# Attention and mixture-of-experts layer on one core: router on centred rows, weight splits behind the slots, zeros ahead of the weights, TensorE on ones while x arrives

## The chip, the cores and the metric

One Trainium2 chip, one of its cores. Its engines run their own instruction streams and wait for each other through semaphores: TensorE (PE; its weight loads PEld), VectorE (DVE), ScalarE (ACT), GpSimd (POOL) and SyncE (SP), which here only issues DMAs. The metric is the device time of one execution in microseconds (us). All numbers below come from the runs and from one profiled execution of this kernel.

## What is computed

x has 8 x 256 tokens of 128 channels, float32. After a layer norm without weights, the result feeds two branches, and the sum goes to the output:

```
xn  = layernorm(x)                                  # (8, 256, 128)
out = x + attn(xn) + ffn(xn)
attn: xq = layernorm(xn) * norm_g + norm_b;  q = xq @ Wq;  k, v = split(xn @ Wkv)
      two null keys and values per head; q, k scaled to length 1 (q_scale, k_scale)
      softmax(8 * q k^T + slope_h * -|i - j|, causal) @ v, 16 heads of 64;  @ Wout
ffn:  shared  = (silu(xn @ sg_w.T) * (xn @ su_w.T)) @ sd_w.T
      probs   = sigmoid(xn @ router_w.T + routing_bias)    # 8 experts
      top 2 per token, weights p / sum(p)
      routed  = sum over the two experts e of w_e * (silu(xn @ wg[e].T) * (xn @ wu[e].T)) @ wd[e].T
```

So there are two norms of tokens: xn (here "first norm", scale `rstd[0]`) and the norm of xn ("second norm", `nmean[1]`, `rstd[1]`).

## The kernel before, in words

Tokens lie on 128 partitions in NT = 16 tiles of 128. The kernel has three parts.

The prologue (0 to about 90 us). SP issues x as one DMA (L316), then wg and wu (L317), wd, the shared weights, Wq, Wkv and Wout, and last three writes of zeros to `slot_x` in DRAM (L328), where each expert's tokens get padded slots. ScalarE's queue issues nine small DMAs counted by one semaphore (`small_in`, L523 to L526; the router's weights and bias are the last two). VectorE takes the mean of x and writes the centred rows `xc` (L713 to L715), ScalarE squares them (L537), VectorE reduces the squares, GpSimd raises the variance to the power -0.5 (L388), VectorE multiplies: `xn1` (L729). In between TensorE transposes the first EARLY = 4 of 14 weight groups (L945), ScalarE writes the rounded high part (L534) and VectorE the rest (L710) of each. TensorE then transposes `xn1` in four groups of four tiles (`tokens_turned`, L949), ScalarE copies them to `xn1T` (L544), and small float32 matmuls with the transposed router weights `rwT` give the logits (`logits`, L957). VectorE adds the bias (L744), ScalarE takes tanh (L548), and a chain of some 60 short VectorE instructions (L747 to L782) finds the two best experts and each token's two places: `slot`; `tile_expert` follows (L784 to L787). TensorE gives the ranks in between (L976, L977).

Then GpSimd scatters the rows of `xn1` to their slots in DRAM with 32 indirect DMAs (`scatter(n)`, L403, loop L498), one after the other on its queue. In front of scatter 15 it waits until the second norm's rows are turned (`t_ev`, L499), and at 15 and 22 it also splits the first 256 tokens of `xn2T` and `xn1T` in two parts (`entry("ahead", ...)`, L445 and L448), from which TensorE computes the first keys and queries ahead (`entry("ahead")`, L1093). The second norm runs on VectorE (L732 to L737) and GpSimd (L392 to L398), and its rows are turned behind the ranks (L978). After that come the null keys and values (L791, L982 to L990, L563 to L565) and the ten other weight groups (L991 on TensorE, L566 on ScalarE, L795 on VectorE), then the subtractions for Wq and Wkv (L798, L799). A group's transposes wait for the evacuation of the group four before it (`w_lo`, L939).

The expert loop (about 90 to 165 us): SP waits for all scatters and for the split of Wq and Wkv (L331, L332), then loads 39 tiles of slots one by one. The batches (the rest): eight passes of 16 heads, on all engines; in each, GpSimd gathers the experts' rows (L494) and scales keys and queries by their norms (L414 to L430).

The semaphore waits that matter: `consts` (GpSimd's constants, 5), `poolc` (its first fills), `rstd_ready`, `xn1_ready`, `slots_ready`, `zero_in`. TensorE's queue is in order: what it does ahead of the tokens, the tokens wait for.

## Time and profile before

| | us |
|---|---|
| median of three runs | 515.41 (513.67 to 516.01) |
| the profiled execution | 515.42 |
| its span (first to last instruction) | 513.7 |

| engine | busy us, share of the span |
|---|---|
| TensorE | 427.9 (83%) |
| VectorE | 374.2 (73%) |
| ScalarE | 356.2 (69%) |
| GpSimd | 327.0 (64%) |

```profile
PE   0557324899998899998998999899899899989985
DVE  3754354465653798788889888888978888897884
POOL 3284787960000598867968968896796888677140
PEclk9997757799999999999999999999999999999999
DMA  7950111222222000001000000100000000010010
```

One digit is the busy share, in tenths, of one of 40 equal slices (12.8 us each). The first seven slices are the prologue, in which no engine but GpSimd is busy for long; the expert loop and the batches follow. PEclk is the granted clock in tenths of full speed, 9 standing for 90% or more; of its two levels, 1.0 is 2.4 GHz and 0.5 is 1.2 GHz. Busy shares are means over stages with different limits, so the prologue is read from the chain of waits and the timelines, whose times count from the span's start. In them "L941" is a line of the kernel, "x16" the number of instructions merged into the row, and the bracket gives the idle time before it and what ended it. GpSimd's times are rough.

### The profile page before, as it was taken

Reading aid. Unit: us, or ns where it says so; the run is one execution under the profiler, and the core shown is the slowest. Engines: PE = TensorE matmul, PEld = TensorE weight load, DVE = VectorE, ACT = ScalarE, POOL = GpSimd, SP = SyncE. Lnnn points to the kernel's source line nnn. Section 1 sums busy time; section 2 is a strip of 40 time slices with the busy share of each in tenths; the row PEclk is TensorE's granted clock in tenths of the full one; section 3 lists DMA queues with packets and bytes.
Section 4 is the critical chain, followed back from the end, with each engine's and each line's share of the span. In section 5 each row is a group of like instructions: output and inputs, shape, how many; then the busy total and the mean of one; then the engine's idle time right before and its main releaser. Section 6 shows DMA issues by size and latency. Waiting matters only on the chain.

```text
span 513.7 us, 11688 instructions
## 1 busy us (share of the span) xinstructions
PE 427.9 (83%) x2793; PEld 305.6 (59%) x2793; DVE 374.2 (73%) x1401; ACT 356.2 (69%) x1091; POOL 327.0 (64%) x492
## 2 busy tenths in 40 slices
PE   0557324899998899998998999899899899989985
PEld 0555212577777566665665666666567566656663
DVE  3754354465653798788889888888978888897884
ACT  1433124466666887886897897889789788869854
POOL 3284787960000598867968968896796888677140
PEclk9997757799999999999999999999999999999999
DMA  7950111222222000001000000100000000010010
GB/s 218 349 156 27 51 36 52 57 76 74 73 79 58 1 1 22 2 3 36 8 0 20 20 0 10 31 0 0 26 15 0 20 20 0 0 36 5 2 42 11
DMA packets 28159, 21.04 MB, mean 41 GB/s; under 512 B 3512, under 2 KB 25312, under 8 KB 28000
## 3 DMA queue, kind: packets, MB, share of 16 engines
q1 hardware_dynamic: 25264, 16.46, 10.8%
q0 software_dynamic: 2048, 4.20, 2.7%
q8 instruction: 13, 0.21, 0.2%
q10 hardware_dynamic: 816, 0.03, 0.1%
q14 instruction: 18, 0.15, 0.1%
HBM read 12.41 MB, written 8.26 MB: 40 GB/s over the span
## 4 chain that ended last, share of the span: by engine, by line
PE 30%; POOL 23%; issue 16%; DVE 14%; ACT 8%; DMA 6%; ACTq 1%; POOLq 1%; SPq 1%; DVEq 1%; another core or an unknown queue 0%
POOL slot_x L404 6%; POOL rnorm L414 4%; PE bank L928 4%; POOL arena_b L494 4%; PE bank L1138 3%; PE bank L929 3%; PE bank L930 3%; DVE arena_b L858 3%; DMA arena_b<-slot_x 3%; DVE arena_b L835 3%; ACT arena_b L646 3%; PE bank L1061 2%; POOL rpow L417 2%; DMA arena_b<-in_L_ffn_wu_dram 2%; PE bank L1070 2%
## 5 line engine op out<-in xcount | busy, mean ns | idle before, releaser
L646 ACT ACTIVATE arena_b<-arena_b,nmx 128x130 f32<-128x130 f32 (+1 forms) x256 | 114.9, 457 | 29.4 <-DVE nmx L858 16.8
L858 DVE CUSTOM_DVE_ANT_0 arena_b<-bank,bias 128x130 f32<-128x130 f32 (+1 forms) x256 | 81.1, 354 | 28.7 <-ACT arena_b L646 14.5
L873 DVE TENSOR_SCALAR arena_b<-arena_b,rden 128x130 f32<-128x130 f32 (+1 forms) x256 | 87.0, 384 | 4.5
L417 POOL TENSOR_TENSOR rpow<-ssm,mhalf 128x8 f32<-128x8 f32 x32 | 53.1, 1659 | 35.2 <-DVE ssm L846 34.5
L1061 PE MATMUL bank<-ident,arena_b 128*128 128x128 f32 x384 | 67.0, 283 | 9.3 <-DVE arena_b L873 9.3
L430 POOL TENSOR_TENSOR arena_b<-arena_b,rnorm 128x512 f32<-128x512 f32 x64 | 66.8, 1044 | 8.4 <-POOL rnorm L420 3.8
L1061 PEld LDWEIGHTS bank<-ident,arena_b 128*128 128x128 f32 x384 | 43.8, 141 | 28.9 <-DVE arena_b L873 20.3
L1070 PE MATMUL bank<-arena_a 64*128 64x130 f32 (+1 forms) x512 | 59.5, 351 | 0.8 <-ACT arena_a L607 0.8
L414 POOL TENSOR_TENSOR rnorm<-ssm,mhalf 128x8 f32<-128x8 f32 x32 | 52.9, 1654 | 0.0
L584 ACT ACTIVATE arena_b<-bank 128x512 f32<-128x512 f32 x64 | 38.1, 595 | 19.7 <-PE bank L930 19.0
L646 ACT ACTIVATION_READ_ACCUMULATOR arena_b<-arena_b,nmx 128x1 f32 x256 | 50.9, 199 | 0.0
L842 DVE TENSOR_REDUCE ssq<-arena_b 128x8 f32<-128x512 f32 x64 | 43.6, 681 | 7.1 <-ACT arena_b L584 5.6
L1016 PE MATMUL bank<-ident,arena_b 128*128 128x128 f32 x256 | 39.8, 279 | 6.9 <-ACT arena_a L593 5.0
L1051 PE MATMUL bank<-probT,arena_a 128*64 128x256 f32 x256 | 43.4, 404 | 2.0 <-ACT oT L626 1.0
L404 POOL DMA_INDIRECT slot_x<-arena_a,slot x32 | 33.2, 1038 | 15.6 <-issue 9.2
L1016 PEld LDWEIGHTS bank<-ident,arena_b 128*128 128x128 f32 x256 | 28.9, 140 | 20.9 <-issue 14.5
L494 POOL DMA_INDIRECT arena_b<-slot_y,slot_now x32 | 32.3, 1010 | 13.8 <-issue 7.3
L1070 PEld LDWEIGHTS bank<-arena_a 64*128 64x128 f32 x512 | 33.6, 186 | 12.4 <-issue 8.9
L883 DVE COPY probT<-bank 128x384 f32<-128x384 f32 x64 | 35.5, 554 | 7.3 <-PE bank L1061 2.3
L445 POOL CAST arena_r<-xn2T 128x256 fp32r (+1 forms) x8 | 3.2, 398 | 56.2 <-PE bank L930 56.2
L1084 PE MATMUL bank<-oT,wo 128*128 128x256 f32 x128 | 38.2, 380 | 0.0
L585 ACT ACTIVATE arena_b<-bank 128x512 f32<-128x512 f32 x64 | 38.0, 593 | 0.0
(202 smaller groups left out, 1032.4 us busy)
## 6 DMA issues: line engine op xcount, KB each, us to landing
slot_x<-probT SPq DMA_DIRECT2D x3, 832.0 KB, 9.9
arena_b<-slot_x SPq DMA_DIRECT2D x39, 64.0 KB, 1.9
slot_y<-arena_b SPq DMA_DIRECT2D x39, 64.0 KB, 1.5
arena_b<-in_L_ffn_wd_dram SPq DMA_DIRECT2D x1, 1024.0 KB, 9.5
arena_b<-in_L_attn_Wkv_dram SPq DMA_DIRECT2D x1, 1024.0 KB, 8.8
arena_b<-in_L_attn_x_dram SPq DMA_DIRECT2D x8, 128.0 KB, 2.1
out_dram<-arena_b SPq DMA_DIRECT2D x8, 128.0 KB, 1.8
arena_b<-in_L_attn_Wq_dram SPq DMA_DIRECT2D x1, 512.0 KB, 6.4
```

The lines of the kernel that those rows point to most:

```text
L404: pool.indirect_dma_start(xg_dram, bass.IndirectOffsetOnAxis(ap=slot[:, n // TOPK, n % TOPK:n % TOPK + 1], axis=0), xn1[:, n // TOPK, :], ...
L414: gp.tensor_tensor(rnorm[:, j, :], ssm[:, j, :], mhalf[:, 0:HEADS // 2], ALU.pow).then_inc(g.r_ready, 1)
L417: gp.tensor_tensor(rpow[:, j, :], ssm[:, j, :], mhalf[:, 0:HEADS // 2], ALU.pow).then_inc(g.pw, 1)
L430: gp.tensor_tensor(rows, rows, bc(rnorm[:, j, :], DH), ALU.mult).then_inc(g.kqn, 1)
L494: pool.indirect_dma_start(yg[:, t, c, :], None, yg_dram, bass.IndirectOffsetOnAxis(ap=slot_now[:, t, c:c + 1], axis=0)).then_inc(g.gath, 16)
L646: sc.activation(prob[:, h % 4, c], sim[h % 2][:, c], ACT.Exp, scale=-1.0, bias=nmx[:, h % HEADS, t:t + 1], accum_out=den[:, h % HEADS, t:t ...
L842: ve.reduce_sum(ssq[j % 2][:], sqb[j % 2].rearrange("p (h d) -> p h d", d=DH), AX.X).then_inc(g.red, 1)
L858: ve.tensor_tensor_reduce(out=sim[h % 2][:, c], in0=bank[h % 2][:, c], in1=bias[:, c], scale=-SLOPES[h], scalar=3e38, op0=ALU.add, op1=ALU ...
L873: ve.tensor_scalar(pr, pr, rden[:, h % HEADS, t:t + 1], None, ALU.mult).then_inc(g.pn, 1)
L1016: ins = te.transpose(side[i][:, q * P:(q + 1) * P], src[:, p * P:(p + 1) * P], ident[:])
L1061: ins = te.transpose(bank[2 + h % 2][:, k * P:(k + 1) * P], prob[:, h % 4, c:c + P], ident[:])
L1070: ins = te.matmul(bank[half][:, c0:c1], qT[r, h // 2, q0:q0 + P], kT[r, h // 2, 0:c1 - c0], start=True, stop=True)
```

## The change

- **x** arrives in two DMAs (tiles 0 to 7, 8 to 15). Behind them SP issues the zero writes and only then the weights. The router's weights are the first small DMA, with their own semaphore; the bias is next among the small ones.
- **Ones.** Before anything else, TensorE runs WARM = 72 bf16 matmuls of the tile `ones` with itself into a bank that nobody reads.
- **Router on centred rows.** Statistics and centring run in halves. TensorE turns `xc` instead of `xn1`, ScalarE copies it to `xn2T` (free at that time), and the router's matmuls have a ninth column of ones, so that the sum of a centred row comes with its logits. VectorE multiplies the sums by `rstd[0]`, adds the bias, and takes the second norm's mean from the ninth column.
- **First norm's rows.** Half 0 on VectorE, half 1 on GpSimd; they are turned after the router and copied to `xn1T` (now evacuations 5 to 8).
- **Second norm.** Its variance is computed on GpSimd; its rows by 16 VectorE instructions with two scalars, into `x_all`; turned last (evacuations 9 to 12).
- **Weights.** All 14 groups are transposed and split behind the slots, the first four included, as are the small steps for the null keys. The null keys' power goes from GpSimd's early part to the place in front of scatter 8. In front of scatter 15, GpSimd waits for evacuation 12 instead of 8.

Context lines are left out; the list of semaphores, too.

```diff
+WARM = 72
...
-rw_raw, rwT = sb("rw_raw", [E, DIM]), sb("rwT", [P, E])
+rw_raw, rwT = sb("rw_raw", [E, DIM]), sb("rwT", [P, E + 1])
...
-sync.dma_start(x_all, xv).then_inc(g.x_in, 16)
+sync.dma_start(x_all[:, 0:NT // 2, :], xv[:, 0:NT // 2, :]).then_inc(g.x_in0, 16)
+sync.dma_start(x_all[:, NT // 2:NT, :], xv[:, NT // 2:NT, :]).then_inc(g.x_in1, 16)
+sync.wait_ge(g.nvz, 1)
+zv = xg_dram.rearrange("(p r) d -> p r d", p=P)
+for i in range(0, SLOT_TILES, 13):
+    sync.dma_start(zv[:, i:i + 13, :], zeros.unsqueeze(1).to_broadcast([P, 13, DIM])).then_inc(g.zero_in, 16)
...
-sync.wait_ge(g.nvz, 1)
-zv = xg_dram.rearrange("(p r) d -> p r d", p=P)
-for i in range(0, SLOT_TILES, 13):
-    sync.dma_start(zv[:, i:i + 13, :], zeros.unsqueeze(1).to_broadcast([P, 13, DIM])).then_inc(g.zero_in, 16)
...
+gp.memset(rwT[:, E:E + 1], 1.0).then_inc(g.poolc, 1)
...
-pool.wait_ge(g.poolc, 27)
+pool.wait_ge(g.poolc, 28)
...
-pool.wait_ge(g.var_ready, 1)
-gp.tensor_tensor(rstd[0][:], var[0][:], mhalf[:, 0:NT], ALU.pow).then_inc(g.rstd_ready, 1)
-pool.wait_ge(g.n_sm, 1)
-gp.tensor_tensor(nr[:], nsm[:], mhalf[0:32, 0:1], ALU.pow).then_inc(g.n_r, 1)
-pool.wait_ge(g.var_ready, 2)
-gp.tensor_tensor(rstd[1][:], var[1][:], mhalf[:, 0:NT], ALU.pow).then_inc(g.rstd_ready, 1)
...
-    gp.tensor_tensor(xc[:, tt, :], xn1[:, tt, :], bc(nmean[1][:, tt], DIM), ALU.add).then_inc(g.xc2_ready, 1)
-    pool.wait_ge(g.xc2_ready, half + 1)
-    pool.wait_ge(g.rstd_ready, 2)
-    gp.tensor_tensor(x_all[:, tt, :], xc[:, tt, :], bc(rstd[1][:, tt], DIM), ALU.mult).then_inc(g.xn2_ready, 1)
+    pool.wait_ge(g.var_ready, half + 1)
+    gp.tensor_tensor(rstd[0][:, tt], var[0][:, tt], mhalf[:, tt], ALU.pow).then_inc(g.rstd_ready, 1)
+tt = slice(NT // 2, NT)
+pool.wait_ge(g.xc1_ready, 2)
+pool.wait_ge(g.rstd_ready, 2)
+gp.tensor_tensor(xn1[:, tt, :], xc[:, tt, :], bc(rstd[0][:, tt], DIM), ALU.mult).then_inc(g.xn1b_ready, 1)
+pool.wait_ge(g.nm2_ready, 1)
+gp.tensor_tensor(vsum[1][:], nmean[1][:], nmean[1][:], ALU.mult).then_inc(g.pchain, 1)
+gp.tensor_tensor(var[1][:], vsum[0][:], rstd[0][:], ALU.mult).then_inc(g.pchain, 1)
+pool.wait_ge(g.pchain, 2)
+gp.tensor_tensor(var[1][:], var[1][:], rstd[0][:], ALU.mult).then_inc(g.pchain, 1)
+pool.wait_ge(g.pchain, 3)
+gp.tensor_scalar(var[1][:], var[1][:], 1.0 / DIM, LN_EPS, ALU.mult, ALU.add).then_inc(g.pchain, 1)
+pool.wait_ge(g.pchain, 4)
+gp.tensor_tensor(var[1][:], var[1][:], vsum[1][:], ALU.subtract).then_inc(g.pchain, 1)
+pool.wait_ge(g.pchain, 5)
+gp.tensor_tensor(rstd[1][:], var[1][:], mhalf[:, 0:NT], ALU.pow).then_inc(g.rstd_ready, 1)
...
+    if n == 8:
+        pool.wait_ge(g.n_sm, 1)
+        gp.tensor_tensor(nr[:], nsm[:], mhalf[0:32, 0:1], ALU.pow).then_inc(g.n_r, 1)
...
-        pool.wait_ge(g.t_ev, 8)
+        pool.wait_ge(g.t_ev, 12)
...
+act.dma_start(rw_raw[:], a["L0_ffn_router_w"]).then_inc(g.rw_in, 16)
...
+act.dma_start(rbias[:], a["L0_ffn_routing_bias"].rearrange("(o e) -> o e", o=1).to_broadcast([P, E])).then_inc(g.small_in, 16)
...
-act.dma_start(rw_raw[:], a["L0_ffn_router_w"]).then_inc(g.small_in, 16)
-act.dma_start(rbias[:], a["L0_ffn_routing_bias"].rearrange("(o e) -> o e", o=1).to_broadcast([P, E])).then_inc(g.small_in, 16)
...
-act.wait_ge(g.xc1_ready, 1)
-sc.activation(sq0, xc, ACT.Square).then_inc(g.sq_ready, 1)
+def squares(half):
+    tt = slice(half * NT // 2, (half + 1) * NT // 2)
+    act.wait_ge(g.xc1_ready, half + 1)
+    sc.activation(sq0[:, tt, :], xc[:, tt, :], ACT.Square).then_inc(g.sq_ready, 1)
+def turned_out(i):
+    act.wait_ge(g.t_ps, i + 1)
+    cols = slice(i % 4 * 512, (i % 4 + 1) * 512)
+    ps = bank[4 + i % 2][:]
+    if i < 8:
+        sc.activation((xn2T if i < 4 else xn1T)[:, cols], ps, ACT.Copy).then_inc(g.t_ev, 1)
+    else:
+        sc.activation(xn2T[:, cols], ps, ACT.Identity, scale=g_col[:, 0:1], bias=b_col[:, 0:1]).then_inc(g.t_ev, 1)
+act.wait_ge(g.rw_ps, 1)
+sc.activation(rwT[:, 0:E], bank[7][:, 0:E], ACT.Copy).then_inc(g.rw_ev, 1)
+squares(0)
+turned_out(0)
+squares(1)
+for i in range(1, 4):
+    turned_out(i)
+act.wait_ge(g.lg_ready, 1)
+sc.activation(lth, lg, ACT.Tanh, scale=0.5).then_inc(g.lth_ready, 1)
+for i in range(4, 8):
+    turned_out(i)
...
-act.wait_ge(g.rw_ps, 1)
-sc.activation(rwT[:], bank[7][:, 0:E], ACT.Copy).then_inc(g.rw_ev, 1)
-for i in range(4):
-    act.wait_ge(g.t_ps, i + 1)
-    sc.activation(xn1T[:, i * 512:(i + 1) * 512], bank[4 + i % 2][:], ACT.Copy).then_inc(g.t_ev, 1)
...
-act.wait_ge(g.lg_ready, 1)
-sc.activation(lth, lg, ACT.Tanh, scale=0.5).then_inc(g.lth_ready, 1)
...
-act.wait_ge(g.small_in, 16 * 9)
-for i in range(4):
-    act.wait_ge(g.t_ps, 4 + i + 1)
-    sc.activation(xn2T[:, i * 512:(i + 1) * 512], bank[4 + i % 2][:], ACT.Identity,
-                  scale=g_col[:, 0:1], bias=b_col[:, 0:1]).then_inc(g.t_ev, 1)
+for n in range(EARLY, len(groups)):
+    split_group(n)
+act.wait_ge(g.small_in, 16 * 8)
+for i in range(8, 12):
+    turned_out(i)
...
-for n in range(EARLY, len(groups)):
-    split_group(n)
...
-dve.wait_ge(g.x_in, 16)
-link(ve.reduce_sum(xsum[0][:], x_all, AX.X))
-link(ve.tensor_scalar(nmean[0][:], xsum[0][:], -1.0 / DIM, None, ALU.mult))
-ve.tensor_tensor(xc, x_all, bc(nmean[0][:], DIM), ALU.add).then_inc(g.xc1_ready, 1)
-dve.wait_ge(g.sq_ready, 1)
-link(ve.reduce_sum(vsum[0][:], sq0, AX.X))
-ve.tensor_scalar(var[0][:], vsum[0][:], 1.0 / DIM, LN_EPS, ALU.mult, ALU.add).then_inc(g.var_ready, 1)
-dve.wait_ge(g.small_in, 16 * 9)
-link(ve.tensor_tensor(nsq[:], nraw[:, 0, :], nraw[:, 0, :], ALU.mult))
-link(ve.reduce_sum(nss[:], nsq[:], AX.X))
-ve.tensor_scalar(nsm[:], nss[:], L2_EPS2, None, ALU.max).then_inc(g.n_sm, 1)
-for n in range(EARLY):
-    split_group(n)
-dve.wait_ge(g.rstd_ready, 1)
-dve.wait_ge(g.xc1_ready, 1)
+for half, arrived in ((0, g.x_in0), (1, g.x_in1)):
+    tt = slice(half * NT // 2, (half + 1) * NT // 2)
+    dve.wait_ge(arrived, 16)
+    link(ve.reduce_sum(xsum[0][:, tt], x_all[:, tt, :], AX.X))
+    link(ve.tensor_scalar(nmean[0][:, tt], xsum[0][:, tt], -1.0 / DIM, None, ALU.mult))
+    ve.tensor_tensor(xc[:, tt, :], x_all[:, tt, :], bc(nmean[0][:, tt], DIM), ALU.add).then_inc(g.xc1_ready, 1)
...
-    ve.tensor_tensor(xn1[:, tt, :], xc[:, tt, :], bc(rstd[0][:, tt], DIM), ALU.mult).then_inc(g.xn1_ready, 1)
-dve.wait_ge(g.xn1_ready, 2)
-link(ve.reduce_sum(xsum[1][:], xn1, AX.X))
-link(ve.tensor_scalar(nmean[1][:], xsum[1][:], -1.0 / DIM, None, ALU.mult))
-link(ve.tensor_tensor(vsum[1][:], nmean[1][:], nmean[1][:], ALU.mult))
-link(ve.scalar_tensor_tensor(out=var[1][:], in0=vsum[0][:], scalar=1.0 / DIM, in1=rstd[0][:], op0=ALU.mult, op1=ALU.mult))
-link(ve.tensor_tensor(var[1][:], var[1][:], rstd[0][:], ALU.mult))
-ve.scalar_tensor_tensor(out=var[1][:], in0=var[1][:], scalar=LN_EPS, in1=vsum[1][:], op0=ALU.add,
-                        op1=ALU.subtract).then_inc(g.var_ready, 1)
-link(ve.tensor_scalar(kdim[:], qsc[:], SIM_SCALE, None, ALU.mult))
-ve.tensor_tensor(kdim[:], kdim[:], ksc[:], ALU.mult).then_inc(g.kdim_ready, 1)
-ve.tensor_copy(nv2[:, 0, :], nraw[:, 1, :]).then_inc(g.n2_ready, 1)
-ve.tensor_copy(nv2[:, 1, :], nraw[:, 1, :]).then_inc(g.n2_ready, 1)
+    dve.wait_ge(g.sq_ready, half + 1)
+    link(ve.reduce_sum(vsum[0][:, tt], sq0[:, tt, :], AX.X))
+    ve.tensor_scalar(var[0][:, tt], vsum[0][:, tt], 1.0 / DIM, LN_EPS, ALU.mult, ALU.add).then_inc(g.var_ready, 1)
+dve.wait_ge(g.rstd_ready, 1)
+dve.wait_ge(g.xc1_ready, 2)
+tt = slice(0, NT // 2)
+ve.tensor_tensor(xn1[:, tt, :], xc[:, tt, :], bc(rstd[0][:, tt], DIM), ALU.mult).then_inc(g.xn1a_ready, 1)
+dve.wait_ge(g.rstd_ready, 2)
...
-ve.tensor_tensor(lg, bank[6][:, 0:NT * E].rearrange("p (t e) -> p t e", e=E), front(rbias[:], NT),
-                 ALU.add).then_inc(g.lg_ready, 1)
+dve.wait_ge(g.small_in, 16 * 8)
+sums = bank[6][:, 0:NT * (E + 1)].rearrange("p (t e) -> p t e", e=E + 1)
+link(ve.tensor_tensor(lgs[:], sums[:, :, 0:E], bc(rstd[0][:], E), ALU.mult))
+ve.tensor_tensor(lg, lgs[:], front(rbias[:], NT), ALU.add).then_inc(g.lg_ready, 1)
+ve.scalar_tensor_tensor(out=nmean[1][:], in0=sums[:, :, E], scalar=-1.0 / DIM, in1=rstd[0][:], op0=ALU.mult,
+                        op1=ALU.mult).then_inc(g.nm2_ready, 1)
...
+for n in range(EARLY):
+    split_group(n)
+link(ve.tensor_tensor(nsq[:], nraw[:, 0, :], nraw[:, 0, :], ALU.mult))
+link(ve.reduce_sum(nss[:], nsq[:], AX.X))
+ve.tensor_scalar(nsm[:], nss[:], L2_EPS2, None, ALU.max).then_inc(g.n_sm, 1)
+link(ve.tensor_scalar(kdim[:], qsc[:], SIM_SCALE, None, ALU.mult))
+ve.tensor_tensor(kdim[:], kdim[:], ksc[:], ALU.mult).then_inc(g.kdim_ready, 1)
+ve.tensor_copy(nv2[:, 0, :], nraw[:, 1, :]).then_inc(g.n2_ready, 1)
+ve.tensor_copy(nv2[:, 1, :], nraw[:, 1, :]).then_inc(g.n2_ready, 1)
+dve.wait_ge(g.rstd_ready, 3)
+dve.wait_ge(g.xn1b_ready, 1)
+dve.wait_ge(g.nm2_ready, 1)
+for t in range(NT):
+    ve.tensor_scalar(x_all[:, t, :], xn1[:, t, :], nmean[1][:, t:t + 1], rstd[1][:, t:t + 1],
+                     ALU.add, ALU.mult).then_inc(g.xn2_ready, 1)
+for n in range(EARLY, len(groups)):
+    split_group(n)
...
-for n in range(EARLY, len(groups)):
-    split_group(n)
...
+pe.wait_ge(g.poolc, 2)
+for _ in range(WARM):
+    te.matmul(bank[3][:, 0:P], ones[:], ones[:], start=True, stop=True)
...
-for n in range(EARLY):
-    transpose_group(n)
-pe.wait_ge(g.small_in, 16 * 9)
+pe.wait_ge(g.rw_in, 16)
...
-    src = xn1 if i < 4 else x_all
+    src = (xc, xn1, x_all)[i // 4]
...
-        ins = te.matmul(bank[6][:, k * E:(k + 1) * E], xn1T[:, k * P:(k + 1) * P], rwT[:], start=True, stop=True)
+        ins = te.matmul(bank[6][:, k * (E + 1):(k + 1) * (E + 1)], xn2T[:, k * P:(k + 1) * P], rwT[:],
+                        start=True, stop=True)
...
-pe.wait_ge(g.xn1_ready, 1)
+pe.wait_ge(g.xc1_ready, 1)
...
-pe.wait_ge(g.xn1_ready, 2)
+pe.wait_ge(g.xc1_ready, 2)
...
+pe.wait_ge(g.xn1a_ready, 1)
+tokens_turned(4)
+tokens_turned(5)
+pe.wait_ge(g.xn1b_ready, 1)
+tokens_turned(6)
+tokens_turned(7)
...
-for i in range(4, 8):
-    pe.wait_ge(g.xn2_ready, i // 2 - 1)
+for n in range(len(groups)):
+    transpose_group(n)
+for i in range(8, 12):
+    pe.wait_ge(g.xn2_ready, 4 * (i - 7))
...
-for n in range(EARLY, len(groups)):
-    transpose_group(n)
```

## Rows read from the trace of the kernel before

**Rows 1.** Chain that ended last, in order of time, first 140 us: start, us, what
```profile
16.05 3.66 PE bank L941 x16
...
29.38 3.23 PE bank L960 x16
...
43.74 1.24 POOL slot_x L404
```

**Rows 2.** Windows: stretch, length, busy us of each engine, granted clock, DMA share, GB/s
```profile
3.00:5.00 2.00, 0.00 (x0) 0.00 (x0) 0.00 (x0) 0.00 (x0) 1.52 (x7) 1.00 0.92 288
...
5.00:7.00 2.00, 0.00 (x0) 0.00 (x0) 0.00 (x0) 0.14 (x1) 0.00 (x0) 1.00 0.95 250
```

**Rows 3.** Timeline of VectorE, first two operations: start, us, operation, count, idle before
```profile
7.62 2.29 DVE L713 TENSOR_REDUCE xsum<-arena_a 128x16 f32<-128x2048 f32 x1 [7.62 <-DMA arena_a<-in_L_attn_x_dram]
...
10.15 2.29 DVE L715 TENSOR_TENSOR arena_a<-arena_a,nmean 128x2048 f32<-128x2048 f32 x1
```

**Rows 4.** Timeline of GpSimd up to 90 us
```profile
17.00 2.94 POOL L388 TENSOR_TENSOR rstd<-var,mhalf 128x16 f32<-128x16 f32 x1 [12.31 <-DVE var L718]
...
19.92 0.55 POOL L390 TENSOR_TENSOR nr<-nsm,mhalf 32x1 f32<-32x1 f32 x1
...
29.64 1.90 POOL L395 TENSOR_TENSOR arena_a<-arena_a,nmean 128x1024 f32<-128x1024 f32 x1
...
62.64 0.41 POOL L445 CAST arena_r<-xn2T 128x256 fp32r<-128x256 f32 x1
...
88.75 1.68 POOL L417 TENSOR_TENSOR rpow<-ssm,mhalf 128x8 f32<-128x8 f32 x1
```

**Rows 5.** Timelines of ScalarE and TensorE, first 45 us
```profile
12.48 1.91 ACT L537 ACTIVATE arena_a<-arena_a 128x2048 f32<-128x2048 f32 x1 [4.33 <-DVE arena_a L715]
...
23.39 0.60 ACT L544 ACTIVATE xn1T<-bank 128x512 f32<-128x512 f32 x1 [2.99 <-PE bank L954]
...
39.73 1.56 ACT L553 ACTIVATE xn2T<-bank,b_col,g_col 128x512 f32<-128x512 f32 x2 [4.66 <-PE bank L954]
...
22.24 1.97 PE L954 MATMUL bank<-ident,arena_a 128*128 128x128 f32 x8 [2.34 <-DVE arena_a L729]
```

**Rows 6.** Timeline of VectorE, 32 to 45 us
```profile
32.63 0.29 DVE L744 TENSOR_TENSOR arena_a<-bank,rbias 128x128 f32<-128x128 f32 x1 [5.43 <-PE bank L960]
...
33.30 0.29 DVE L747 TENSOR_SCALAR arena_a<-arena_a 128x128 f32<-128x128 f32 x1 [0.38 <-ACT arena_a L548]
...
44.59 0.37 DVE L787 CAST tile_expert<-tef 128x39 int32<-128x39 f32 x1
```

**Rows 7.** Timelines of VectorE and GpSimd beside each other, scatters and batch loop
```profile
69.14 2.28 DVE L799 TENSOR_TENSOR wkv_lo<-arena_b,wkv_hi 128x2048 fp32r<-128x2048 f32 x1
...
69.23 3.04 POOL L404 DMA_INDIRECT slot_x<-arena_a,slot  x1 [0.30 <-issue]
...
304.83 0.55 DVE L873 TENSOR_SCALAR arena_b<-arena_b,rden 128x130 f32<-128x130 f32 x2
...
317.15 2.10 DVE L835 SCALAR_TENSOR_TENSOR arena_b<-arena_b,w_now 128x128 f32<-128x128 f32 x4 [0.17 <-DVE arena_b L828]
...
318.06 1.04 POOL L430 TENSOR_TENSOR arena_b<-arena_b,rnorm 128x512 f32<-128x512 f32 x1 [0.16 <-POOL rnorm L414]
```

**Rows 8.** Weight groups: VectorE by line, timelines of VectorE and TensorE, one window
```profile
L707 DVE COPY ed<-bank 128x512 f32<-128x512 f32 x4 | 2.8, 691 | 7.9 <-PE bank L941 4.3 <-remote 3.5
...
51.51 0.69 DVE L710 TENSOR_TENSOR egu_lo<-bank,egu_hi 128x512 fp32r<-128x512 f32 x1 [0.81 <-issue]
...
60.86 0.69 DVE L707 COPY ed<-bank 128x512 f32<-128x512 f32 x1 [2.16 <-PE bank L941]
...
67.67 0.42 DVE L710 TENSOR_TENSOR sd_lo<-bank,sd_hi 128x256 fp32r<-128x256 f32 x1 [0.52 <-issue]
...
55.13 1.46 PE L941 MATMUL bank<-ident,arena_b 128*128 128x128 f32 x8 [0.71 <-issue]
...
52.00:54.00 2.00, 1.99 (x17) 1.64 (x16) 1.55 (x3) 1.17 (x3) 1.51 (x2) 0.99 0.11 37
```

6 lines of the change are left out of this document (4 added, 2 removed).

## The prediction

> **What bounds the kernel now.** I read the page first, then the chain of waits over the first 140 us, then the timelines of VectorE, GpSimd, ScalarE and TensorE up to the expert loop. The page shows no bottleneck engine for the whole span; the chain shows what the prologue hangs on. In it, TensorE waits for the weights wg and wu (16.05 us), turns them, then the tokens wait for that, and the 32 little router matmuls end at 32.6 us; 43.74 us is the first scatter [rows 1]. From there 32 scatters run one after the other on GpSimd to 88.7 us [rows 4], and the expert loop can't start before the last one has landed. VectorE, ScalarE and TensorE have gaps during all of this. So the time is: start of the first scatter, plus some 45 us of GpSimd queue, plus a rest (experts and eight batches) that the diff leaves alone. The change is worth what it moves the first scatter, minus what it adds to GpSimd's queue between scatter 0 and scatter 31.
>
> **x comes in two halves.** x is 1.05 MB. The windows give 288 GB/s from 3 us and 250 GB/s after [rows 2]: half of x is moved by 4.8 us, all of it by 6.9 us. The first reader started at 7.62 us [rows 3], 0.7 us behind the bytes, so the first half is usable at 5.5 us. The three zero writes now follow x on SP's queue in place of wg; what follows x is different, not more, so I take the second half at 7.6 us as before. Every weight waits behind the zeros: 2.6 MB at 300 GB/s or so is 8.5 us, which puts wg and wu near 24 us. VectorE's first split is now at 30 us, so this is hidden; if it were not, it would cost what the splits come late. The total of bytes is the same.
>
> **Statistics.** VectorE: the reduction and the subtraction take 2.29 us each for 2048 columns [rows 3], so about 1.2 us for a half. With the small step between (0.2 us): centred half 0 at 8.1, half 1 at 10.8 us. ScalarE's square is 1.91 us whole [rows 5], 1.0 us a half: half 0 done by 10, half 1 at 11.9. VectorE reduces the squares 10.85 to 12.0 and 12.1 to 13.3, variance ready at 12.2 and 13.45. The power on 16 columns took 2.94 us, on 8 columns 1.68 us [rows 4]: GpSimd ends at 13.9 and 15.6 us.
>
> **Router on centred rows.** It no longer waits for the power or for the weights. ScalarE copies four banks (0.60 us each [rows 5]): the second at 12.4 behind the square of half 1, the last at 14.2 if TensorE is quick, 15.0 if slow. Then four matmuls. TensorE turned 8 tiles in 1.97 us before, 0.23 us each [rows 5], and the 16 last router matmuls took 3.23 us, 0.20 us each [rows 1]. At that pace the router sums are complete at 16.0 us. [...]
>
> **A collision that the change creates.** At 15.6 us GpSimd starts the normalisation of half 1, 1.9 us for 128x1024 [rows 4], and VectorE starts the multiplication of the logits. The next VectorE instruction adds the bias with both inputs in SBUF (before, one was in PSUM [rows 6]). What such a pair does stands in the batch loop: four VectorE instructions with two SBUF inputs each took 2.10 us together, where four of the 128x130 kind beside them would take 1.1, and they ended only after GpSimd's 1.04 us multiplication at 318.06 had ended [rows 7]. So I let the bias wait for GpSimd: ready at 17.9 instead of 16.3 us. The Trainium skill, "SBUF — State Buffer", section "Who interferes with whom", says that a VectorE instruction with two SBUF inputs and a GpSimd one that reads SBUF exclude each other for the whole instruction. By that rule, too, it is 1.6 us; the trace agrees.
>
> **From the logits to the first scatter.** Before: logits added at 32.63, next step at 33.30, scatter at 43.74 [rows 1, 6]: 10.44 us, unchanged in the diff. After: next step at 18.25, first scatter at 28.7 us. GpSimd's second statistics (five small ones and a 2.9 us power) end near 22.5 us and are hidden, as the zeros are. **The first scatter moves by 15.0 us.**
>
> **GpSimd's queue between the scatters.** New there: the null keys' power, 0.55 us [rows 4], with its gap 0.65 us, on the path in full. The VectorE step it needs is done by 34 us, it stands at 39. The 16 normalisations on VectorE (two of 130 and 258 columns take 0.55 us [rows 7], so some 0.21 each) are 3.4 us; I take no cost for the scatters beside them. One scatter took 3.04 instead of 0.96 us, beside the 2.28 us subtraction of wkv [rows 7]. That subtraction still falls among the scatters, so this stays; between 2 us less and 1.2 us more, by where a scatter begins.
>
> **The wait in front of scatter 15.** It stood at 62.64 us [rows 4], for evacuations that were over 19 us earlier. Now it is for the twelfth evacuation, behind all 14 weight groups, and 17 scatters queue behind it. Due: 28.7 + 18.9 + 0.65 = 48.25 us. The chain: slots' last step 29.95 (before 44.59 + 0.37 [rows 6]), four splits at 0.66 to 32.6, small ones to 33.8, normalisations to 37.2, ten splits at 0.69 [rows 8] with TensorE at 0.9 us a group (four of the 0.23 us) to 44.0, four token groups to 46.9 us (each evacuation 0.78 us [rows 5]). That is in time by 1.3 us. But before, the same ten groups took from 51.51 to 68.09 us, 16.6 us where I count 6.8, and VectorE stood idle for 7.9 us in front of the four copies of ed, put down mostly to TensorE, although TensorE's rows show their transposes issued by 56 us [rows 8]. I can't explain these 9.8 us; they fell inside the scatters. Taken at 0, the wait costs nothing; at 9.8, it costs 8.5. New here is that the chain also contains the groups behind. I take half, 4.9 us late, so 3.6 us of stall.
>
> What follows TensorE's last token group (null keys, wo, the subtractions for Wq and Wkv) is needed at the latest when GpSimd has split the second rows at scatter 22. That comes seven scatters and one split, over 10 us, behind the wait; I estimate that work at some 9 us from its place before, and a little more is covered too, because the last scatter is released by none of it. The last scatter stays last.
>
> **Sum.** 15.0 - 0.65 - 3.6 = 10.75 us less. The profiled execution took 515.42 us (span 513.7, 1.7 us around it), the median is 515.41, so no correction: 504.6 us, span 502.9.
>
> **Rivals.** (A) As above, 504.6 us. (B) The weight chain is in time: 501.1. For it, every instruction in the chain is short and TensorE has been warmed; against it, the unexplained 9.8 us. (C) Besides, bias and GpSimd don't collide: 499.5. Against it stand rows 7. (D) The 9.8 us come back whole: 509.5. (E) The wait in front of scatter 15 turns the gain over. The six groups from the first copy of ed and the four token groups, ten in all, start at 37.9 us; if each goes at the pace of the third copy of ed before (2.16 us idle and 0.69 us busy [rows 8]), the wait ends at 66.4 us, 3.8 us behind 62.64, and the kernel takes 519.2. It decides from 2.5 us a group. Against it: before, only some groups were so slow; ten took 16.6 us. (F) The ones don't raise TensorE's clock: sums at 16.0, 0.4 us worse, 505.0; with the 72 taking 7.7 us. Alone this changes little, because the power is nearly as late.
>
> **How the numbers follow.** A 0.42, B 0.20, C 0.08, D 0.20, E 0.04, F 0.06. The range goes from C to a little beyond D, 499.5 to 510.5, which leaves out E and tails of D. 0.5% (2.6 us) is about what a measurement can tell from no change. All but E are faster by more than that; with a D that grows, I give faster 0.92, same 0.04, slower 0.04.
>
> **What would show it.** First scatter near 28.7 us (27.1 without the collision); the bias addition ends with GpSimd's normalisation at 17.6; first half read at 5.5; rstd complete at 15.6, router sums before it; between scatter 14 and 15 an idle GpSimd whose releaser is ScalarE; TensorE's first transposes 0.11 us apart. The prediction is wrong if the scatters stop for something else (weights landing late, the descriptors of the zeros), or if x's second half lands after 9 us behind the zeros.

## The result and the profile after

| us | before | after |
|---|---|---|
| median | 514.95 (513.67 to 516.01, 4 runs) | 506.02 (505.49 to 506.59, 4 runs) |
| the profiled execution | 515.42 | 505.49 |
| its span | 513.7 | 503.8 |
| first scatter starts | 43.74 | 28.30 |
| last scatter starts | 87.77 | 75.84 |
| from there to the end of the span | 425.9 | 428.0 |

The ratio of the medians is 0.983, interval 0.980 to 0.986: 8.9 us less. The forecast was 504.6, with the first scatter at 28.7 us and a stall of 3.6 us in front of scatter 15. GpSimd's timeline of the kernel after, the rows to hold against [rows 4] and the first scatter of [rows 1]:

```profile
28.30 1.23 POOL L416 DMA_INDIRECT slot_x<-arena_a,slot  x1 [6.18 <-DVE slot L800]
...
47.05 0.96 POOL L416 DMA_INDIRECT slot_x<-arena_a,slot  x1 [0.30 <-issue]
51.36 0.40 POOL L457 CAST arena_r<-xn2T 128x256 fp32r<-128x256 f32 x1 [3.35 <-ACT xn2T L563]
...
56.67 1.45 POOL L416 DMA_INDIRECT slot_x<-arena_a,slot  x1 [0.30 <-issue]
58.42 1.89 POOL L416 DMA_INDIRECT slot_x<-arena_a,slot  x1 [0.31 <-issue]
...
75.84 0.97 POOL L416 DMA_INDIRECT slot_x<-arena_a,slot  x1 [0.30 <-issue]
```

The reader is to see three things: the start of the queue, the idle 3.35 us in front of L457 (the new wait, in front of scatter 15), and two scatters longer than 0.97 us, which stand beside the subtractions for Wq and Wkv on VectorE:

```profile
56.05 1.22 DVE L831 TENSOR_TENSOR wq_lo<-arena_b,wq_hi 128x1024 fp32r<-128x1024 f32 x1
57.20 2.28 DVE L832 TENSOR_TENSOR wkv_lo<-arena_b,wkv_hi 128x2048 fp32r<-128x2048 f32 x1
```

From first to last scatter it is 47.54 us, before it was 44.03. The 3.51 us more are, by the starts of the scatters, the stall (3.35), the null keys' power (0.59) and longer scatters 4 to 6 beside VectorE's normalisations (0.22), less 0.67 because the two subtractions now cost 0.48 + 0.92 us of scatters, one each, where Wkv's alone cost 2.07 before and Wq's nothing.

TensorE and VectorE of the kernel after, the start of the router, against the PE rows of [rows 1, 5] and the DVE rows of [rows 3, 6]:

```profile
1.34 6.87 PE L979 MATMUL bank<-ones 128*128 128x128 bf16 x72 [1.34 <-POOL ones L366]
8.30 1.09 PE L989 MATMUL bank<-ident,arena_a 128*128 128x128 f32 x8
12.30 1.06 PE L995 MATMUL bank<-rwT,xn2T 128*128 128x9 f32 x8 [0.62 <-ACT xn2T L561]
13.68 3.28 PE L995 MATMUL bank<-rwT,xn2T 128*128 128x9 f32 x16
```

```profile
4.74 1.22 DVE L743 TENSOR_REDUCE xsum<-arena_a 128x8 f32<-128x1024 f32 x1 [4.74 <-DMA arena_a<-in_L_attn_x_dram]
7.98 1.22 DVE L743 TENSOR_REDUCE xsum<-arena_a 128x8 f32<-128x1024 f32 x1 [0.56 <-DMA arena_a<-in_L_attn_x_dram]
17.06 0.29 DVE L760 TENSOR_TENSOR lgs<-bank,rstd 128x128 f32<-128x128 f32 x1 [2.03 <-PE bank L995]
17.38 0.29 DVE L761 TENSOR_TENSOR arena_a<-lgs,rbias 128x128 f32<-128x128 f32 x1
```

Eight transposes take 1.09 us (1.97 before), so the ones did raise the clock. But the last 16 router matmuls take 3.28 us, 0.20 each, as before. The windows (span from:to, busy time and instructions of the engines, then the granted clock) say why:

```profile
7.10:13.90 6.80, 5.42 (x56) 4.84 (x53) 5.63 (x9) 4.52 (x8) 1.81 (x2) 0.99 1.16 340
13.90:20.70 6.80, 6.73 (x31) 5.96 (x30) 4.37 (x38) 2.64 (x6) 5.91 (x8) 0.50 1.07 311
```

The clock is at the upper level (2.4 GHz) to 13.9 us and at the lower (1.2 GHz) behind, and the sums that I put at 14.8 us are complete at 17.0.

What stands behind the stall, ScalarE and TensorE of the kernel after:

```profile
42.61 0.60 ACT L549 ACTIVATE sgu_hi<-bank 128x512 fp32r<-128x512 f32 x1 [6.28 <-PE bank L974]
44.02 0.38 ACT L549 ACTIVATE sd_hi<-bank 128x256 fp32r<-128x256 f32 x1 [0.81 <-remote]
45.51 0.78 ACT L563 ACTIVATE xn2T<-bank,b_col,g_col 128x512 f32<-128x512 f32 x1 [1.11 <-remote]
47.60 0.78 ACT L563 ACTIVATE xn2T<-bank,b_col,g_col 128x512 f32<-128x512 f32 x1 [1.31 <-PE bank L989]
49.74 1.45 ACT L563 ACTIVATE xn2T<-bank,b_col,g_col 128x512 f32<-128x512 f32 x2 [1.37 <-PE bank L989]
```

```profile
41.75 1.04 PE L989 MATMUL bank<-ident,arena_a 128*128 128x128 f32 x8
46.44 0.63 PE L989 MATMUL bank<-ident,arena_a 128*128 128x128 f32 x4 [3.65 <-ACT xn2T L563]
```

The first two groups of tokens were issued between 41.75 and 42.8 us, yet ScalarE could only take the first at 45.51 and the second at 47.60. This is the picture of [rows 8] again (transposes issued, their reader idle for microseconds more), now in front of the wait. The granted clock was 1.00 from 41.2 to 48.0 us, so it isn't the clock.

### The profile page after: what moved, and what is told of

It reads as the page before. It is cut to its first block, busy times and chain, and to the rows that moved or that the text cites. A ratio compares the mean times of both kernels' runs of the same rounds, so it can differ in the third digit from the quotient of the medians.

```text
span 503.8 us, 11892 instructions
## 1 busy us (share of the span) xinstructions
PE 435.0 (86%) x2881; PEld 313.6 (62%) x2881; DVE 374.0 (74%) x1417; ACT 358.5 (71%) x1096; POOL 322.7 (64%) x496
## 4 chain that ended last, share of the span: by engine, by line
PE 31%; POOL 20%; issue 16%; DVE 15%; ACT 9%; DMA 5%; ACTq 1%; POOLq 1%; DVEq 1%; another core or an unknown queue 0%; SPq 0%
POOL rnorm L426 5%; PE bank L961 4%; POOL arena_b L506 4%; PE bank L963 4%; PE bank L1179 3%; POOL slot_x L416 3%; PE bank L962 3%; DMA arena_b<-slot_x 3%; DVE arena_b L891 3%; DVE arena_b L868 3%; PE bank L1102 2%; PE bank L1111 2%; ACT arena_b L674 2%; POOL rpow L429 2%; DVE arena_b L906 2%
## 5 line engine op out<-in xcount | busy, mean ns | idle before, releaser
L891 DVE CUSTOM_DVE_ANT_0 arena_b<-bank,bias 128x130 f32<-128x130 f32 (+1 forms) x256 | 81.0, 354 | 28.7 <-ACT arena_b L674 14.6
L1092 PE MATMUL bank<-probT,arena_a 128*64 128x256 f32 x256 | 43.4, 404 | 2.0 <-ACT oT L654 1.0
L457 POOL CAST arena_r<-xn2T 128x256 fp32r (+1 forms) x8 | 3.2, 398 | 61.5 <-PE bank L963 58.2
```

What stands on the lines that cost most here:

```text
L891: ve.tensor_tensor_reduce(out=sim[h % 2][:, c], in0=bank[h % 2][:, c], in1=bias[:, c], scale=-SLOPES[h], scalar=3e38, op0=ALU.add, op1=ALU ...
```

## The experiments

The runs came in three groups, each on one chip of its own and with runs of the kernel before beside it: median before 512.5 us in the first group (no_ones to collide), 511.2 in the second (before_again to fill_apart), 511.6 in the third (norm_late to together_no_ones). The record doesn't name the chip of the result above. I take it for a fourth, because its median before is higher (514.95) and a batch takes 43.7 us in both of its traces and 43.4 or 43.5 in all twelve others. Four runs are single executions: hold_at_8, collide, before_again and zeros_last. Times are compared within a group, or as ratios; starts in the prologue agree well enough between chips to be compared directly.

The theories: the first scatter hangs on the router sums and on GpSimd's normalisation beside them; the queue of scatters passes on every microsecond; the wait in front of scatter 15 costs what the weight chain is late. The rivals: the ones do nothing; the collision isn't one; the lateness belongs to the execution and not to the order of the work.

**No ones.** `WARM = 72` becomes 0.

```diff
-WARM = 72
+WARM = 0
```

> The changed kernel without the 72 matmuls on ones. Theory (the ones lift TensorE's clock early and nothing more): the eight transposes of the first two token groups go back from 0.14 to 0.23 us apart, the router sums, complete at 17.06 us with the ones, come 0.5 to 1.5 us later, and so does the first scatter (28.3 us with the ones); the time rises by the same, to about 507 us. Rival (the ones are worth little, because the clock had fallen again by 13.9 us and the last sums ran at the low level anyway): sums and first scatter within 0.4 us, time within 0.1%.

498.49 us (497.76 to 499.3), ratio 0.973 (0.971 to 0.975). TensorE of this run:

```profile
7.43 1.97 PE L989 MATMUL bank<-ident,arena_a 128*128 128x128 f32 x8 [2.38 <-DVE arena_a L745]
14.94 3.42 PE L995 MATMUL bank<-rwT,xn2T 128*128 128x9 f32 x16
```

The slow pace from the first transposes on; sums read at 18.45 us, first scatter at 29.81, so 1.5 us later than in the profiled execution of the kernel after (not in every execution of it, as the next runs show). The windows show a granted clock of 1.00 for this run up to 52 us, although eight transposes took 1.97 us at 7.43 and 1.04 us at 43.62: ahead of its first change, that figure doesn't tell the level, and the pace of the matmuls does. The first three slices of PEclk of the kernel before are of this kind: they show 9, and the eight transposes at 22.24 took 1.97 us. And no stall: L457 starts at 49.52, as soon as scatter 14 ends; the four token groups' evacuations stand in one row, 44.36, 3.04 us for four, all in time. Against the expected 507 us the time is 8.5 us less, so this run says nothing of what the ones are worth in time.

**The wait four scatters later.** The wait for the twelfth evacuation and the first split stand in front of scatter 19, the second split in front of 24.

```diff
-if n == 15:
+if n == 19:
     pool.wait_ge(g.t_ev, 12)
-if n in (15, 22):
-    entry("ahead", -1, [n // 22])
+if n in (19, 24):
+    entry("ahead", -1, [n // 24])
```

> The changed kernel with the wait for the twelfth evacuation and the row splits at scatters 19 and 24 instead of 15 and 22. Theory (the 3.35 us of idle GpSimd in front of scatter 15 is on the path): no idle there, last scatter ends 3.3 us earlier (at 73.5 us), time 502.7 us. Rival (something else, such as TensorE's keys and queries ahead or the null chain, is as late as the scatters): the expert loop begins less than 1 us earlier, time above 505 us.

499.43 us (497.12 to 499.67), ratio 0.973 (0.971 to 0.976): the same as without ones. In this execution, too, the chain was in time (no idle GpSimd), so nothing was there to be saved. The last scatter starts at 73.50 us, the very figure expected, but by another way: from a first scatter at 29.73. With ones in place its sums were read at 18.49 us, no earlier than without: the clock had fallen at 11.2 us, before the second group of router matmuls began.

**Scatters held at 8.** The same wait stands in front of scatter 8 as well.

```diff
 if n == 8:
+    pool.wait_ge(g.t_ev, 12)
     pool.wait_ge(g.n_sm, 1)
```

> The changed kernel with the wait for the twelfth evacuation in front of scatter 8 already, so that no indirect DMA is issued between 38.6 us and the end of the weight chain. It costs time on purpose. [...] It gives a price, though: GpSimd idle for 7.02 us in front of its power (L514), the last scatter at 80.65 us instead of 74.36 (no ones) or 73.50 (wait at 19), the time 9.4 or 8.4 us longer. The last scatter is 6.3 or 7.2 us later and nothing of it comes back behind it, so a stall of the queue is paid in full.

**The collision made.** GpSimd's normalisation of half 1 waits for the router sums, so that both start together.

```diff
 pool.wait_ge(g.rstd_ready, 2)
+pool.wait_ge(g.lg_ps, 4)
```

> The changed kernel with GpSimd's normalisation of half 1 held until the router sums are complete, so that it starts together with VectorE's multiplication of the logits. Theory (a VectorE instruction with two SBUF inputs waits for a GpSimd one that reads SBUF): the bias addition, 0.29 us long and ended at 17.67 us, ends only when GpSimd is done, at about 19.1 us, and the first scatter comes 1.3 to 1.6 us later. Rival (no exclusion for these two): bias addition 0.29 us, first scatter at 28.3 us.

498.18 us. GpSimd and VectorE of this run:

```profile
16.99 1.89 POOL L399 TENSOR_TENSOR arena_a<-arena_a,rstd 128x1024 f32<-128x1024 f32 x1 [1.55 <-PE bank L996]
```

```profile
17.23 1.80 DVE L762 TENSOR_TENSOR arena_a<-lgs,rbias 128x128 f32<-128x128 f32 x1
```

The bias addition takes 1.80 instead of 0.29 us and ends with GpSimd (19.03, against 18.88); the first scatter comes at 29.77 us, 1.5 later than at 28.30 although the sums were read 0.15 us earlier. The collision is real and has the forecast's size; in the kernel after it doesn't happen, because the sums come when GpSimd is nearly done (17.43 us).

**Both kernels again**, on another chip, with no edit.

> The kernel before, unchanged, profiled beside the changed one on the same chip. In the first profile of it the four copies of ed stood 2.8 to 4.2 us apart, because TensorE's results were signalled late among the scatters. Theory (that lateness belongs to some executions or chips, not to the kernel): here the copies are 0.7 to 0.9 us apart, and the weight chain from the first split of the fifth group to the last split takes 8 us instead of 16.6. Rival (it belongs to the kernel): 16 us again.

> The changed kernel, unchanged. Theory (the lateness of TensorE's signals in its first profile belongs to the execution or the chip, and cost 3.35 us in front of scatter 15 there): no idle in front of scatter 15, first scatter between 28.3 and 29.8 us by the phase of the clock, last scatter near 74 us, time 13 to 14.5 us below the kernel before. Rival (the kernel itself makes it late): idle of 3 us there again and a gain of 9 us.

Before 512.08 in that execution (511.2 the median of its group), after 499.72 (497.88 to 502.08; 501.53 in the profiled execution), ratio 0.976 (0.970 to 0.981). VectorE of the kernel before, repeated, where [rows 8] had 2.16 us of idle time before one copy:

```profile
50.24 2.48 DVE L710 TENSOR_TENSOR egu_lo<-bank,egu_hi 128x512 fp32r<-128x512 f32 x4 [0.35 <-ACT egu_hi L534]
52.64 2.48 DVE L707 COPY ed<-bank 128x512 f32<-128x512 f32 x4
```

Ten groups take 5.8 us where they took 16.6, 1.0 us from the 6.8 that I had counted. The 9.8 unexplained microseconds belonged to that execution or its chip. The kernel after, repeated, has no stall (L457 at 48.34, scatter 14's end). Its first two token groups on TensorE and all four evacuations on ScalarE:

```profile
41.77 1.04 PE L989 MATMUL bank<-ident,arena_a 128*128 128x128 f32 x8
```

```profile
42.51 3.04 ACT L563 ACTIVATE xn2T<-bank,b_col,g_col 128x512 f32<-128x512 f32 x4
```

The pace is the full clock's, and scatters are issued beside them all the while. So the theory behind the run with the scatters held at 8, that scatters and the full clock together make TensorE's results late, can't be the whole cause. The repetition the two subtractions elsewhere. GpSimd and VectorE:

```profile
48.94 1.80 POOL L460 TENSOR_TENSOR arena_r<-xn2T,arena_r 128x256 fp32r<-128x256 f32 x1 [0.18 <-POOL arena_r L457]
50.90 2.86 POOL L416 DMA_INDIRECT slot_x<-arena_a,slot  x1 [0.16 <-issue]
```

```profile
48.92 1.23 DVE L831 TENSOR_TENSOR wq_lo<-arena_b,wq_hi 128x1024 fp32r<-128x1024 f32 x1
50.07 2.82 DVE L832 TENSOR_TENSOR wkv_lo<-arena_b,wkv_hi 128x2048 fp32r<-128x2048 f32 x1
```

The split waits for Wq's subtraction, Wkv's for the split (2.82 instead of 2.28 us), and scatter 15 for Wkv's: 3.0 us on the path together, 1.8 in the repeated before. First scatter 28.63, last 74.34, against 43.27 and 87.12.

**Zeros behind the weights.** SP issues the three zero writes after all weights again.

```diff
-sync.wait_ge(g.nvz, 1)
-zv = xg_dram.rearrange("(p r) d -> p r d", p=P)
-for i in range(0, SLOT_TILES, 13):
-    sync.dma_start(zv[:, i:i + 13, :], zeros.unsqueeze(1).to_broadcast([P, 13, DIM])).then_inc(g.zero_in, 16)
...
 sync.dma_start(wo[:], a["L0_attn_Wout"].rearrange("(c p) d -> p c d", p=P)).then_inc(g.o_in, 16)
+sync.wait_ge(g.nvz, 1)
+zv = xg_dram.rearrange("(p r) d -> p r d", p=P)
+for i in range(0, SLOT_TILES, 13):
+    sync.dma_start(zv[:, i:i + 13, :], zeros.unsqueeze(1).to_broadcast([P, 13, DIM])).then_inc(g.zero_in, 16)
```

> The changed kernel with the three zero writes back behind all weight loads on SP's queue. Theory (the zeros have to be ahead once the slots are ready this early): they land near 33 us as in the kernel before, so the first scatter waits for them until 33.2 us instead of 28.3 to 29.8, 3.5 to 5 us of time lost; the second half of x lands within 0.4 us of 8.0. Rival (the zeros hinder x and gain nothing): x half 1 over 0.5 us earlier, first scatter not later than 30 us.

505.66 us, one execution. GpSimd:

```profile
34.48 1.32 POOL L416 DMA_INDIRECT slot_x<-arena_a,slot  x1 [10.49 <-DMA slot_x<-probT]
```

The slots were ready at 29.9 us, but the first scatter waits for the zeros to 34.48, 4.6 us, and the last is at 79.77. The second scatter (36.10) takes 2.57 us here, beside the sixteen normalisations on VectorE (34.52 to 38.70), which have one input of data and cost only 0.2 us of scatters elsewhere. This move was not a side matter: before, the zeros landed some 10 us ahead of need; with the first scatter 15 us earlier they would be the next bound, and the change would give some 6 us less (505.66 against 499.72).

**Ones between the groups.** 30 more tiles of ones, 12, 4, 10 and 4, stand between TensorE's token groups and router matmuls, and GpSimd's normalisation of half 1 waits for the bias addition.

```diff
+pool.wait_ge(g.lg_ready, 1)
...
 tokens_turned(1)
+fill(12)
 pe.wait_ge(g.rw_ev, 1)
 logits(0)
+fill(4)
 pe.wait_ge(g.xc1_ready, 2)
 tokens_turned(2)
+fill(10)
 logits(1)
 tokens_turned(3)
+fill(4)
 logits(2)
```

> The changed kernel with 30 more matmuls on ones between the token groups and router matmuls, so that TensorE is busy until the last router sum, and with GpSimd's normalisation of half 1 held until the logits are complete, so that it doesn't meet the bias addition. Theory (clock at its upper level through the sums, and no collision): sums complete at 15.9 us at the latest, logits at 16.4, first scatter at 26.9 us, that is 1.4 to 2.9 us earlier than in the changed kernel, and the time lower by as much. Rival (the added matmuls delay the tokens as much as the clock gives): first scatter not before 28 us.

498.25 us (497.51 to 503.76), ratio 0.977 (0.970 to 0.984). TensorE's last 16 router matmuls, then VectorE:

```profile
13.88 1.91 PE L1000 MATMUL bank<-rwT,xn2T 128*128 128x9 f32 x16
```

```profile
15.87 0.29 DVE L761 TENSOR_TENSOR lgs<-bank,rstd 128x128 f32<-128x128 f32 x1 [0.87 <-PE bank L1000]
16.20 0.29 DVE L762 TENSOR_TENSOR arena_a<-lgs,rbias 128x128 f32<-128x128 f32 x1
16.87 1.78 DVE L766 TENSOR_SCALAR arena_a<-arena_a 128x128 f32<-128x128 f32 x1 [0.29 <-ACT arena_a L574]
```

The clock now holds through the router (1.00 from 7 to 16 us): 0.11 us a matmul, sums read at 15.87. But the first scatter is at 28.75, no earlier than in the two executions of the kernel after (28.30 and 28.63). The gain of 1.5 us at the sums (17.37 in the repetition) ended in a collision that neither my theory nor this edit had foreseen: the scaling of the logits, with a single input in SBUF, takes 1.78 instead of 0.26 us beside GpSimd's normalisation (16.67 to 18.57). By the Trainium skill, "SBUF — State Buffer", section "Who interferes with whom", `tensor_scalar` can take both port pairs in its fast mode, and then it and GpSimd exclude each other, the one that issues first holding the shared pair for its whole instruction; this row agrees, GpSimd having started 0.2 us ahead.

**The normalisation behind the small steps.** As the last, but GpSimd's normalisation of half 1 stands behind the five small steps of the second statistics, in front of their power, without the wait for the bias.

```diff
-tt = slice(NT // 2, NT)
-pool.wait_ge(g.xc1_ready, 2)
-pool.wait_ge(g.rstd_ready, 2)
-gp.tensor_tensor(xn1[:, tt, :], xc[:, tt, :], bc(rstd[0][:, tt], DIM), ALU.mult).then_inc(g.xn1b_ready, 1)
...
 gp.tensor_tensor(var[1][:], var[1][:], vsum[1][:], ALU.subtract).then_inc(g.pchain, 1)
+tt = slice(NT // 2, NT)
+pool.wait_ge(g.xc1_ready, 2)
+pool.wait_ge(g.rstd_ready, 2)
+gp.tensor_tensor(xn1[:, tt, :], xc[:, tt, :], bc(rstd[0][:, tt], DIM), ALU.mult).then_inc(g.xn1b_ready, 1)
 pool.wait_ge(g.pchain, 5)
```

> The change with 30 more tiles of ones between the groups of tokens, as in the run with ones between the groups, and with GpSimd's normalisation of half 1 behind its five small statistics steps instead of in front of them. Theory (hold by ports): the ones bring the router sums to about 15.9 us; what took that back was VectorE's scaling of the logits (128x128, one input in SBUF), 1.78 instead of 0.26 us beside GpSimd's normalisation. Now the normalisation runs beside the sixteen MAX8 and FIND_INDEX8 and holds nothing: scaling 0.26 us, first scatter 27.2 us, last scatter near 71. Rival (any VectorE instruction is held): the first MAX8 or FIND_INDEX8 takes 1.5 us more and the first scatter stays at 28.7 us. Median 496.7 by the theory, 498.2 by the rival: a difference that the trace shows and the median hardly.

496.94 us (496.85 to 497.66), ratio 0.972 (0.969 to 0.975). VectorE and GpSimd:

```profile
17.08 0.27 DVE L765 TENSOR_SCALAR arena_a<-arena_a 128x128 f32<-128x128 f32 x1 [0.29 <-ACT arena_a L573]
17.38 1.19 DVE L767 MAX8 arena_a<-arena_a 128x8 f32<-128x8 f32 x16
```

```profile
18.11 1.90 POOL L408 TENSOR_TENSOR arena_a<-arena_a,rstd 128x1024 f32<-128x1024 f32 x1
27.46 1.23 POOL L416 DMA_INDIRECT slot_x<-arena_a,slot  x1 [4.60 <-DVE slot L800]
```

The scaling is back at 0.27 us. The sixteen MAX8 take 1.19 us as always, the last of them beside the normalisation, and so do the FIND_INDEX8 that follow beside it (0.16 us each); the first scatter comes at 27.46, 1.3 us earlier. The rival (everything on VectorE is held) is out.

**Wkv's subtraction in four.**

```diff
-ve.tensor_tensor(wkv[1][:], raw_w[:, INNER:3 * INNER], wkv[0][:].bitcast(F32), ALU.subtract).then_inc(g.wraw_lo, 1)
+for c in range(0, 2 * INNER, 512):
+    i = ve.tensor_tensor(wkv[1][:, c:c + 512], raw_w[:, INNER + c:INNER + c + 512], wkv[0][:, c:c + 512].bitcast(F32), ALU.subtract)
+i.then_inc(g.wraw_lo, 1)
```

> The change with VectorE's subtraction for Wkv cut from one instruction of 2048 columns into four of 512. Theory (GpSimd's issue of a scatter waits for the running VectorE instruction and comes in at its end): a scatter or split beside it takes at most 0.7 us more than 0.97; the excess of all long scatters and splits together, 3.0 us in the repeated trace of the change and 1.9 in the one without ones, is 0.6 to 1.5 us. Rival (VectorE keeps the hold through a row of such instructions): one scatter still takes 2.9 us or two take 1.9. Median 1 us below the change's by the theory, the same by the rival; the scatters' durations decide.

499.84 us (497.5 to 501.44), ratio 0.976 (0.973 to 0.979): in time no better than the kernel after. GpSimd's scatters, then VectorE's subtractions for Wkv:

```profile
50.81 1.80 POOL L416 DMA_INDIRECT slot_x<-arena_a,slot  x1 [0.16 <-issue]
52.91 1.47 POOL L416 DMA_INDIRECT slot_x<-arena_a,slot  x1 [0.30 <-issue]
```

```profile
51.65 2.48 DVE L833 TENSOR_TENSOR wkv_lo<-arena_b,wkv_hi 128x512 fp32r<-128x512 f32 x4
```

The first scatter was held by Wq's subtraction (50.41 to 51.73), which had stayed whole, and ends 0.88 us behind its end; the second ends at 54.38, 0.87 us behind the end of the third quarter (53.51), not behind the fourth. So a scatter gets in between two VectorE instructions. A gain isn't shown: the two cost 1.3 us more than free ones, and with Wkv's subtraction whole the scatters and splits beside the pair cost between 1.0 us (wait_at_19, fill_apart) and 3.0 us (after_again), by where a scatter happened to begin. Cutting can only take away the worst of these cases.

**Everything together**, and the same without any tile of ones. The edits are those above: ones between the groups, the normalisation behind the small steps, Wkv in four, the wait at 19 and the second split at 24; the other run has `WARM = 0` and no fills.

> The change with all that helped or could: ones between the groups, normalisation of half 1 behind the small steps, Wkv's subtraction in four, the wait for the twelfth evacuation in front of scatter 19 instead of 15 and the second rows in front of 24. If the first scatter's place, the long scatters and the wait are what the time hangs on: first scatter 27.2, last scatter 70 to 71, no idle GpSimd between them, median 495.5 (494 to 498), 0.968 of the kernel before. If the rest behind the last scatter (422 to 428 us in the traces so far) hangs on something else, such as the clock's turn at the start of the loops, the median stays at 498 although the last scatter is at 71.

> As the run with everything together, but without any tile of ones. Theory that the ones are worth what they bring the sums forward: sums 18.4 instead of 15.9 us, first scatter 29.7 instead of 27.2, last scatter 73, median 2.5 us above the other's. Rival (the ones only move the turns of the clock, and give back in the expert loop or the batches what they win at the start): the median is within 1 us of the other's, and its rest behind the last scatter is some 2 us shorter.

With ones 496.05 us (495.18 to 498.88), ratio 0.971 (0.968 to 0.974); without 499.67 (497.99 to 500.71), 0.976 (0.974 to 0.979). First scatters at 27.20 and 29.71 us, last at 70.55 and 72.97. GpSimd of the first:

```profile
27.20 1.23 POOL L416 DMA_INDIRECT slot_x<-arena_a,slot  x1 [4.60 <-DVE slot L800]
...
48.47 1.57 POOL L416 DMA_INDIRECT slot_x<-arena_a,slot  x1 [0.30 <-issue]
```

Only one scatter is still held, by 0.6 us (by Wq's subtraction). The ones are worth 2.5 us at the first scatter once they hold the clock up to the end of the router, and 2.4 us of it are left at the last. The medians are 3.6 us apart, in the same direction; the intervals just overlap, and 1.2 us of the difference is in the rest (below). The run no_ones at the head of this section, with none of the other edits, has 0.973; so the medians don't show that the other edits gain anything without the ones.

**The rest behind the last scatter.** The prediction left it unchanged. The traces have 422.4 to 428.0 us. Up to the first gathers of the batches it varies between 106 and 110 us; what differs is TensorE's wait for the rows of the slots in the expert loop. The waits of TensorE over 63 us of that loop, in the kernel after, its repetition and the run without ones (us in total, times, longest):

```profile
PE bank L1153 <- DMA arena_b<-slot_x: 4.4, 4, 1.3
```

```profile
PE bank L1153 <- DMA arena_b<-slot_x: 3.1, 4, 1.6
```

```profile
PE bank L1153 <- DMA arena_b<-slot_x: 0.6, 1, 0.6
```

Their rests are 428.0, 425.5 and 422.7; the two executions of before have 1.9 (425.9) and 1.2 us (423.2). Taking the waits off, the twelve traces read in this way (all but hold_at_8 and zeros_last) lie between 421.6 and 424.0 us, the two highest being those of the first pair's chip, where a batch takes 43.7 us instead of 43.4. Why some loads come late in one execution and not in the next, no run here tells. It falls in kernels of both kinds, over 2 us in five of ten with the change and in neither of the two of before, which is too few to call it an effect.

## Why the prediction was right, step by step

- **x, statistics, powers.** First half read at 4.74 instead of 5.5 us, second at 7.98 instead of 7.6, powers done at 15.4 instead of 15.6: right.
- **Router sums.** Wrong: 14.8 forecast, 17.0 measured, and two steps failed. The first is "Then four matmuls": four router matmuls are eight rows of the trace, and the last two token groups, sixteen rows, run behind the last transposes. They take 1.91 us at the higher level (fill_apart) and 3.42 at the lower (no_ones), so the sums come at 15.87 even with the clock held up, and at 18.45 instead of 16.0 without ones. The second is that the ones decide only 0.4 us, which took the clock, once up, as staying up. In the seven traces with the 72 ones alone it fell between 11.2 and 14.1 us (13.9 here, 13.5 in the repetition, 11.2 with the wait at 19), and the sums were read between 16.91 and 18.94 us; in four of the seven (18.36 to 18.94) no earlier than without ones (18.45 and 18.34). So the 72 ones alone may give nothing. I had no case in which the sums came last by over 1 us.
- **The collision.** Right as a mechanism, not as an event: the forced one cost 1.5 us of the 1.6 forecast, but in the kernel after the late sums stepped out of its way. Two misses of opposite sign and like size, which is luck: the bias addition ended at 17.67 us, forecast 17.9.
- **Logits to first scatter.** 10.44 us forecast from the next step, 10.25 measured (18.05 to 28.30): right.
- **Zeros.** Hidden, as said; behind the weights they would have cost 4.6 us at the first scatter.
- **GpSimd's queue.** The power put 0.59 us between the scatters, forecast 0.65. The 16 normalisations took 4.23 us, not 3.4, and lengthened scatters by 0.22. The subtractions came out 0.7 us cheaper in the first pair, 1.2 us dearer in the second (3.0 against 1.8), by where a scatter begins: at the bounds given (2 less to 1.2 more). That Wq's holds a scatter too, the sum had not.
- **The wait in front of scatter 15.** 3.35 us of stall against 3.6, but the lateness sat elsewhere than in the weight chain of before: the ten groups' last split ended at 44.85, forecast 44.0, and the four token groups, forecast done at 46.9, ended at 51.2. In the executions on the other chips the stall is nought, as rival B has it. Taking half of an unexplained 9.8 us was a guess between two cases, that it came near 3.35 is luck, and each of the cases exists; the repetition of before shows that the 9.8 us were no property of the kernel alone.
- **Sum.** First scatter 15.44 us earlier, stall 3.35, power 0.59, scatters 4 to 6 0.22, the subtractions 0.67 back: the last scatter is 11.95 earlier by this sum, 11.93 by the rows. The rest takes 2.1 back, which had no term; the waits for slot rows are 2.5 us longer. 9.9 us for the profiled pair, 10.75 forecast. For the profiled pair of the second group it was 10.55 (512.08 to 501.53): 14.64 at the first scatter, 12.78 at the last, 2.3 given back in the rest; its medians are 11.5 apart (511.2 to 499.72).

What stays open: why TensorE's results were signalled microseconds late in both profiled executions of the first chip and in none of the twelve on the three others, and why loads of slot rows are late. The run with the scatters held at 8 was to test the first and met no lateness. No run takes back the router on centred rows, or the weight splits behind the slots, alone; that the 15 us at the first scatter come from them is read from the order of the rows, and how they share it isn't shown. The fastest version is the one with everything together: 496.05 us, 0.971 of before, not to be told from the one with the normalisation late (0.972).

## What to carry to other kernels

Idle time that the order of the work doesn't explain may belong to one execution: repeat the profile of the kernel before, on another chip too, before half of it goes into a sum. Keeping TensorE busy ahead of its work pays only if it stays busy up to the end of that work; fill the gaps between its groups, and look at the pace of the matmuls and the granted clock at the end of the stretch, not at its start. When a step on VectorE moves earlier, look at what GpSimd does at the new time, and give GpSimd its wide two-input step beside MAX8 and FIND_INDEX8, not beside additions and scalings.

## What the runs showed of the hardware that I had not expected

- Scaling 128x128 float32 values with one input in SBUF took 1.78 instead of 0.26 us beside GpSimd's 128x1024 multiplication; MAX8 and FIND_INDEX8 beside the same took their usual time (norm_late). So did two-input instructions beside GpSimd's power: in norm_late the power runs from 19.96 to 22.86 us, and VectorE's two 128x128 comparisons (L776) take 0.49 us from 21.23.
- GpSimd's issue of a scatter is held by VectorE instructions with two inputs in SBUF: 2.86 and 3.04 instead of 0.96 us. In all fourteen traces a scatter held by the subtraction for Wq or Wkv ends 0.8 to 0.9 us behind the end of the VectorE instruction, and one that began just ahead of it (67.96 beside Wq's at 68.01, before) took its 0.97. The page named above infers that `tensor_tensor` doesn't hold the issue of descriptors; for these scatters, which also read their places from `slot`, the rows speak against it, and the measurement decides.
- TensorE's clock fell at times between 11.2 and 14.1 us in seven executions with the same TensorE instructions up to there, and the sums came up to 2 us apart; with the 30 tiles between the groups it was up to the end of the router in all three traces that had them.
- The same float32 transposes, all issued within 1.04 us at full clock, could be read up to 3 us and more after their issue in one execution (45.51 for those begun at 41.75) and at once in others.
